# Narrow attentions of a six-block decoder: one pair of first scores in every step, the preparation turned by half a period, and the row maxima handed on in three groups

## The reference

```python
q, k = rope(x @ Wq), rope(src @ Wk)          # 32 heads of 16; 8 key heads (self) or 32 (cross)
s = q @ k.T                                  # 256 x 256 for each head; causal in self
attn = softmax(s / 4) @ (src @ Wv)
x = layernorm(x + attn @ Wo)                 # cross: + bout
```

## Time and profile before

| | |
|---|---|
| median of three runs | 3,955.1 us |
| profiled execution, device time | 3,946.1 us |
| its span in the profile | 3,944.4 us |
| granted clock of TensorE, mean over the span | 0.933 |
| TensorE matmuls busy | 3,485.5 us, 88% |
| VectorE busy | 1,760.1 us, 45% |
| ScalarE busy | 1,233.8 us, 31% |
| GpSimd busy | 287.2 us, 7% |
| the narrow attentions | from about 2,060 to 3,245 us of the span |

### The profile page before, as it was taken

How to read it: one execution, slowest core, us unless ns; L and a number is a source line. 1 busy time by engine, 2 the same in 40 slices (tenths; PEclk the granted TensorE clock), 3 DMA queues, 4 the chain that set the end, 5 groups by cost and what they waited for, 6 DMA issues and landing times. The chain is left out here.

```text
span 3944.4 us, 53071 instructions
## 1 busy us (share of the span) xinstructions
PE 3485.5 (88%) x18713; PEld 2422.7 (61%) x18714; DVE 1760.1 (45%) x5074; ACT 1233.8 (31%) x2714; POOL 287.2 (7%) x317
## 2 busy tenths in 40 slices
PE   7899999989999999977947898988888865999996
PEld 7666777756777777753424555544444434777774
DVE  4433444435444444431154545555555546334445
ACT  1222333323333333332112333334434434122111
POOL 2222000011000000023130000000000000000000
PEclk8999999999999999978967998999988877999998
DMA  6511111122111111123440000000000001000001
GB/s 238 187 38 38 53 48 48 45 94 86 46 45 43 45 45 45 32 111 135 133 133 1 2 2 2 18 10 18 4 5 7 1 25 41 11 21 11 11 21 43
DMA packets 83092, 191.62 MB, mean 49 GB/s; under 512 B 23424, under 2 KB 27520, under 8 KB 81864
## 3 DMA queue, kind: packets, MB, share of 16 engines
q0 software_dynamic: 32912, 100.03, 8.2%
q1 hardware_dynamic: 50048, 89.82, 6.6%
HBM read 138.30 MB, written 50.47 MB: 48 GB/s over the span
## 5 line engine op out<-in xcount | busy, mean ns | idle before, releaser
L1762 DVE TENSOR_REDUCE mx_n<-bank 128x6 f32<-128x768 f32 (+1 forms) x256 | 279.8, 1093 | 234.9 <-PE bank L1542 142.6
L1673 ACT ACTIVATE probsT_n<-bank 128x768 f32<-128x768 f32 (+1 forms) x256 | 235.9, 921 | 352.5 <-PE bank L1561 196.2
L1536 PE MATMUL bank<-kT_n,qT_n 48*128 48x256 f32 (+1 forms) x1024 | 143.4, 362 | 133.7 <-DVE mx_n L1762 131.5
L447 PE MATMUL bank<-wo_s,work_s 128*128 128x512 f32 x512 | 229.0, 598 | 6.3 <-ACT work_s L479 3.8
L447 PE MATMUL bank<-wo_x,work_x 128*128 128x512 f32 x512 | 227.2, 594 | 5.0 <-ACT work_x L479 3.8
L1536 PEld LDWEIGHTS bank<-kT_n,qT_n 48*128 48x128 f32 x1024 | 89.7, 213 | 211.8 <-DVE mx_n L1762 138.9
L479 ACT ACTIVATE work_s<-bank 128x512 f32<-128x512 f32 (+1 forms) x224 | 104.2, 465 | 353.9 <-PE bank L436 174.1
L479 ACT ACTIVATE work_x<-bank 128x256 f32<-128x256 f32 (+1 forms) x240 | 109.6, 460 | 322.6 <-PE bank L436 188.4
L584 DVE CUSTOM_DVE_ANT_0 work_x<-bank,work_x 128x256 f32<-128x256 f32 x256 | 97.8, 419 | 220.7 <-issue 220.7
L525 ACT ACTIVATE work_x<-work_x 128x256 f32<-128x256 f32 x256 | 128.3, 502 | 196.0 <-DVE work_x L589 196.0
L584 DVE CUSTOM_DVE_ANT_0 work_s<-bank,const 128x128 f32<-128x128 f32 (+1 forms) x256 | 80.8, 353 | 214.7 <-issue 214.7
(11 more groups left out here) (375 smaller groups left out, 7100.1 us busy)
## 6 DMA issues: line engine op xcount, KB each, us to landing
wq_lo_s<-wq_lo_s POOLq DMA_DIRECT2D x64, 512.0 KB, 3.6
wq_lo_x<-wq_lo_x POOLq DMA_DIRECT2D x64, 512.0 KB, 3.5
expert_rows<-table_zero SPq DMA_DIRECT2D x20, 512.0 KB, 14.2
work_m<-expert_rows SPq DMA_DIRECT2D x40, 256.0 KB, 2.6
expert_products<-work_m POOLq DMA_DIRECT2D x40, 256.0 KB, 2.7
expert_table<-table_zero SPq DMA_DIRECT2D x16, 512.0 KB, 14.1
weights_m<-expert_table SPq DMA_DIRECT2D x4, 2048.0 KB, 9.6
ug_rows<-in_L_ffn_W_gate SPq DMA_DIRECT2D x9, 512.0 KB, 3.6
```

The costliest lines, as they stand in the source:

```text
L447: last = pe.matmul(out[t][:, :], oT[:, h, t * P:(t + 1) * P], wo[:, h, :], start=(h == 0), stop=(h == H - 1), skip_group_check=True)
L1536: last = pe.matmul(out, q, kT[half(h, ROWS), n % 2, key_block(n, h), 0:keys], start=(t == 0), stop=cross(n), skip_group_check=True)
L1673: act.activation(probsT[:, turn_ % SLOT_PAIRS, :, 0:cols], scoreT[:, :, 0:cols], ACT.Exp, scale=SCALE)\
L1762: dve.tensor_reduce(to.rearrange("p t h -> p h t"), seen, AX.X, ALU.max).then_inc(s["scores_read"], 1)
```

## The change

`step` is rewritten. First scores: step `at` < 8 has pair `at` + 8 of the **current** item, step `at` >= 8 has pair `at` - 8 of the next one, so every step has one pair. Preparation moves about half an item: q, qT, kT11, kT12, kT13 and v of item n + 1 stay in item n, at steps 0 to 10; xT, ctxT, k, and the kT of item n + 2 now stand in steps 10 to 15 of item n. out0 and out1 of the last item move from steps 8 and 9 to 4 and 6, the norm stages from 10 to 13 to 7 to 10. The maxima go in three groups: pairs 0 to 5 (negA, step 14), 6 to 9 (negB, step 2 of the item), 10 to 15 (negC, step 8 of the item, first used in step 10). The prologue becomes seven units and 16 steps of an item -1, without second scores and values. The wait for the bias moves from VectorE's start to where it is used.

```diff
-        if at == 2:
-            a.append(("negB", n))
-        if g is not None:
-            whole = [x for x in ("kT02", "kT03", "kT12", "kT13") if cross(g)]
-            a += [(x, g) for x in {3: ["kT01"] + whole[0:1], 4: ["q0"] + whole[1:2], 5: ["kT11"] + whole[2:3],
-                                   6: ["qT00", "qT01"], 7: ["qT03", "qT10"], 10: ["qT12"], 11: ["v0"], 12: ["qT13"],
-                                   13: ["negA"]}.get(at, [])]
-            b += [(x, g) for x in {0: ["k0"], 1: ["k1"], 2: ["kT00"], 4: ["kT10"], 5: whole[3:4] + ["q1"], 6: ["qT02"],
-                                   7: ["qT11"], 12: ["v1"]}.get(at, [])]
-            if at >= 8:
-                a.insert(0, (2 * (at - 8), g))
-                b.insert(0, (2 * (at - 8) + 1, g))
...
+    GROUPS = ((0, 6), (6, 10), (10, PAIRS))
...
+        if at < 8:
+            put(a, now, [at + 8])
+        else:
+            put(a, g, [at - 8])
+        if at == 0:
+            put(a, f, ["h0", "h2"])
+            put(a, g, ["kT11"])
+            put(b, g, wide(g, "kT12", "kT13"))
+            put(b, g, ["q0"])
+        elif at == 1:
+            put(a, f, ["h1", "h3"])
+        elif at == 2:
+            put(a, now, ["negB"])
+            put(b, f, wide(f, "hT0", "hT1"))
+        elif at == 3:
+            put(a, g, ["q1"])
+        elif at == 4:
+            put(b, f, ["out0"])
+        elif at == 5:
+            put(a, g, ["qT00"])
+            put(b, g, ["qT01"])
+        elif at == 6:
+            put(b, f, ["out1"])
+        elif at == 7:
+            put(a, g, ["qT10"])
+            put(b, g, ["qT11", "qT02"])
+        elif at == 8:
+            put(a, now, ["negC"])
+            put(b, g, ["qT03", "qT12"])
+        elif at == 9:
+            put(a, g, ["v0"])
+            put(b, g, ["qT13"])
+        elif at == 10:
+            put(a, g, ["v1"])
+            put(b, e, ["xT0"])
+        elif at == 11:
+            put(a, e, ["xT1"])
+            put(b, e, wide(e, "ctxT"))
+        elif at == 12:
+            put(a, e, ["k0"])
+        elif at == 13:
+            put(a, e, ["k1"])
+        elif at == 14:
+            put(a, g, ["negA"])
+            put(b, e, ["kT00"])
+        elif at == 15:
+            put(a, e, ["kT01"])
+            put(a, e, wide(e, "kT02"))
+            put(b, e, wide(e, "kT03"))
+            put(b, e, ["kT10"])
...
+    before = [(x, 0) for x in ("xT0", "xT1", "k0", "k1", "kT00", "kT01", "kT10")]
...
-    mx, neg_hl = sb("mx", [P, 3, NH]), sb("neg_hl", [P, 2, TILES, 2, NH // 2])
-    negT = sb("negT", [P, 2, SEQ], FP32R)
+    mx, neg_hl = sb("mx", [P, 3, 3 * 12]), sb("neg_hl", [P, 3, TILES, NH])
+    negT = sb("negT", [P, 3, SEQ], FP32R)
...
-                for i, name in enumerate(("negA", "negB")):
+                for i, (name, (lo, hi)) in enumerate(zip(GROUP_NAMES, GROUPS)):
...
-                if pair % 8 == 0:
-                    pe.wait_ge(s["negA_there" if pair == 0 else "negB_there"], 64 * (n + 1))
+                if pair in (lo for lo, _ in GROUPS):
+                    pe.wait_ge(s[f"{GROUP_NAMES[group_of(pair)]}_there"], 64 * (n + 1))
...
-                if pair % 8 == 7:
-                    negate(n, pair // 8)
+                if pair == hi - 1:
+                    negate(n, i, 2 * other)
...
+            dve.memset(neg_hl[:, :, :, :], 0.0)
...
-                    if n >= 1 and at in (10, 11, 12, 13):
-                        norm_stage(at - 10, n - 1)
+                    if n >= 1 and at in (7, 8, 9, 10):
+                        norm_stage(at - 7, n - 1)
```

More of the change, by code:

```diff
@@ L1346, in attention_narrow @@
     turns = lambda n: range(4 if cross(n) else 2)
+    GROUPS = ((0, 6), (6, 10), (10, PAIRS))
+    GROUP_NAMES = ("negA", "negB", "negC")
+    group_of = lambda pair: [i for i, (lo, hi) in enumerate(GROUPS) if lo <= pair < hi][0]
     def step(n, at):
         f = n - 1 if n >= 1 else None
+        now = n if n >= 0 else None
         g = n + 1 if n + 1 < ITEMS else None
@@ L1371, in step @@
-        if e is not None:
-            a += [(x, e) for x in {14: ["xT0"]}.get(at, [])]
-            b += [(x, e) for x in {14: ["xT1"], 15: ["ctxT"] if cross(e) else []}.get(at, [])]
-        return a, b
[L1376 to L1379, removed]
@@ L1380, in attention_narrow, with put @@
-    after = order(ITEMS - 1, ["h0", "h2", "h1", "h3", "hT0", "hT1", "out0", "out1"])
-    whole = before + [u for n in range(ITEMS) for at in range(PAIRS) for slot in step(n, at) for u in slot] + after
+        def put(slot, item, names):
+            if item is not None:
+                slot.extend((x, item) for x in names)
+        wide = lambda item, *names: names if item is not None and cross(item) else ()
+        if at < 8:
+            put(a, now, [at + 8])
+        else:
+            put(a, g, [at - 8])
@@ L1382, in attention_narrow @@
+        return a, b
+    before = [(x, 0) for x in ("xT0", "xT1", "k0", "k1", "kT00", "kT01", "kT10")]
+    after = [(x, ITEMS - 1) for x in ("h0", "h2", "h1", "h3", "hT0", "hT1", "out0", "out1")]
+    whole = before + [u for n in range(-1, ITEMS) for at in range(PAIRS) for slot in step(n, at) for u in slot] + after
     uses = PrepOrder([u for u in whole if isinstance(u[0], str)])
@@ L1515, in prepare @@
                 else:
-                    i = "AB".index(name[3])
-                    pe.wait_ge(s["neg_ready"], 2 * n + i + 1)
+                    i = GROUP_NAMES.index(name)
+                    pe.wait_ge(s["neg_ready"], 3 * n + i + 1)
                     for t in range(TILES):
-                        last = pe.transpose(b[0:NH, t * P:(t + 1) * P],
-                                            neg_hl[:, i, t, :, :].rearrange("p l h -> p (l h)"), chip.ident)
+                        last = pe.transpose(b[0:NH, t * P:(t + 1) * P], neg_hl[:, i, t, :], chip.ident)
                 last.then_inc(s["prep_ready"], 1)
@@ L1617, in _ @@
                 emit(name, n)
-            for n in range(ITEMS):
+            for n in range(-1, ITEMS):
                 for at in range(PAIRS):
-                    second_scores(n, at)
+                    if n >= 0:
+                        second_scores(n, at)
                     early, late = step(n, at)
@@ L1687, in _ @@
                 evacuate(name, n)
-            for n in range(ITEMS):
+            for n in range(-1, ITEMS):
                 for at in range(PAIRS):
-                    exponentials(n, at)
+                    if n >= 0:
+                        exponentials(n, at)
                     early, late = step(n, at)
@@ L1843, in _ @@
                 do(name, n)
-            dve.wait_ge(s["bias_loaded"], 16)
-            for n in range(ITEMS):
+            for n in range(-1, ITEMS):
                 for at in range(PAIRS):
```

30 lines of the change are left out of this document (15 added, 15 removed).

## The result

| | before | changed |
|---|---|---|
| median of four runs, us | 3,954.5 | 3,847.7 |
| range, us | 3,944.4 to 3,961.7 | 3,835.6 to 3,849.6 |
| profiled execution, us | 3,946.1 | 3,847.9 |

A forecast was written before the change was run, and what follows sets the result against it. TensorE bounds the kernel, idling for the maxima and losing clock. Items 0 to 14 gain 92 us, with the prologue 109; 3,946.1 less 109 is 3,837, put at 3,840; range 3,805 to 3,875, with both neighbours 3,785 to 3,895.

The forecast's parts named there:

- Items 0 to 14: Steady part of the stage: 960 us against 1,052, a gain of 92 us.
- The walk of the waits: One pair per step, waits for maxima followed step by step: stalls 6.7 us per cross item; periods 64 cross, 59.5 self.
- The groups: Three groups of maxima, twelve row DMAs per item instead of eight: 0.3 us a mean item, bounds 0 and 1.5.
- The rest of the stage: Item 15 gets eight pairs of scores, taken to lie under its exponentials: 0 to +2 us.
- The prologue: Eight of sixteen pairs go, eight steps of some 3 us at low clock; item 0 starts near 2112: 17 us gained.
- The clock: TensorE's clock in the items: one fall per cross item, +4 us, and 1 us on a self item.
- That the clock stays up: Rival, chance 0.20: spread-out waits never lower TensorE's clock; gain 145 us, 3,801 us.
- VectorE as the pacemaker: Rival, chance 0.17: rotations between maxima delay everything behind, clock falls twice; self 64, cross 72; gain 54, 3,892 us.
- Slower: Rival, chance 0.03: waits of steps 2, 3, 14 and 15 keep the clock at 1.2 GHz; +97, 4,043 us.
- That it would not do what it says: Rival, chance 0.05: waits only change places, item times as now, the prologue alone gains; 3,929 us.
- The signs: Steady part: maxima wait 55 to 80 us, items about 60 and 68, clock above 0.91, item 0 near 2112.
- The sign of a low stretch over 13 us: Listed as showing the forecast wrong: stretches at low clock longer than 13 us.

The follow-up runs named there:

- e7_late: Changed kernel with the first scores of steps 2, 14 and 15 issued behind other units of the step; ratio 0.9772, 3,855.1 us.
- e8_late_split: Changed kernel with first scores late in steps 2, 14 and 15 and VectorE's rotations split around the next maxima; ratio 0.9796, 3,867.9 us.
- e2_two_groups: Changed kernel with the maxima handed on in two groups of eight pairs, negA in step 15, no negC; ratio 1.0235, 4,025.7 us.
- e1_pairs_only: Changed kernel keeping one pair per step and three groups, but preparation, out0/out1 and norm stages placed as before the change; ratio 0.9775, 3,841.7 us.
- e4_fill: Changed kernel with extra transposes rewriting the same values just ahead of the two long waits; ratio 0.9659, 3,794.9 us; repeated on another chip, 0.9683.
- e3_split: Changed kernel with VectorE's rotation split: bank-freeing multiplies, then the next step's maxima, then the rest; ratio 0.9682, 3,808.5 us.
- e5_split_after: Changed kernel with rotations split, the rest done behind the next step's maxima and other early units; ratio 0.9695, 3,827.7 us.

## Why the prediction was right, point by point

Forecast 3,840 us, in the range 3,785 to 3,895; measured 3,847.7. The terms:

- **Items 0 to 14**: forecast 960 us, measured 960. That it fits to the microsecond is luck. Items 0 to 5 took 369 us (forecast 363), items 6 and 7 134 (131), items 8 to 13 397 (408), item 14 61 (58): 12 us too little in one part and 11 too much in the other. It was also set against 1,052 us, where items 0 to 14 of the kernel before take 1,055.8 up to item 15's first second scores; the gain there is 96 us where 92 was forecast.
- **The walk of the waits** (part 1) was the step that carried it. Cross: forecast 2.6, 0.8 and 2.8 us in steps 2, 14 and 15, measured 2.95, 1.07 and 2.58. The 0.3 us in step 3 did not come in cross items. Self: forecast 1.8, 1.0 and 0.35, measured 1.78, 0.78 and 0.66; of the 0.55 us for negA's rows nothing came. The sum over items 0 to 14 was to be 55 to 80 us and is 70.6.
- **The groups** (part 3): twelve row DMAs an item cost nothing in the steady part, 0.4 us in one wait. The forecast 0.3 us an item was a little high. The Trainium skill (DMA: Bandwidth & Descriptors, Anatomy of one DMA) tells its fixed cost of some 2.0 us for the path through GpSimd, where these DMAs are issued by SyncE; worked out from it, as an estimate, 6 us more would have gone off the gain, and no steady item shows that wait. A wait for the rows does show twice at the end, at the start of item 15 and in its step 10:

```profile
3078.58 0.69 PE L1593 MATMUL bank<-qT_n,kT_n 50*128 50x256 f32 x4 [2.83 <-DMA qT_n<-negT_n]
...
3110.81 0.80 PE L1593 MATMUL bank<-qT_n,kT_n 50*128 50x256 f32 x4 [2.83 <-DMA qT_n<-negT_n]
```

- **The rest of the stage**: item 15 was forecast at 0 to +2 us, and the rest came out 8.9 us longer. The step that failed was to take the eight pairs of first scores as lying under the exponentials. TensorE's work there, at full clock, grew by 2.5 us, idle time by 3.1 us, nearly all of it the wait of step 10 for negC's rows, and low busy time by 6.8 us, half of which is 3.4. The cover of the DMAs had been counted in the steady part only: with no item left to prepare, steps 8 and 9 of item 15 have no qT and v units, and steps 14 and 15 of item 14 no kT units, so negC's and negA's rows are each waited for 2.83 us. (negA's wait ends where item 15 begins and counts with items 0 to 14.)
- **The prologue** (part 4) was mis-sized: forecast 17 us gained, measured 25.4. I priced the eight steps at the low clock of the old prologue's pairs, some 3 us each, 26 us. They took 19.8 us (2,098.77 to 2,118.59), the first six some 2 us each, and the clock there is 1.00 where it was 0.50 (a window of each, before and changed):

```profile
2100.00:2120.00 20.00, 11.40 (x54) 5.33 (x52) 8.22 (x11) 0.00 (x0) 0.00 (x0) 0.50 0.00 0
...
2100.00:2110.00 10.00, 8.96 (x77) 7.28 (x76) 5.67 (x11) 3.43 (x7) 0.00 (x0) 1.00 0.00 0
```

  In the old prologue TensorE waited for the maxima between the pairs (16.1 us in 15 waits); in the new one v, xT and k lie between them. Of the 25.4 us, 13.4 are idle time and 11.0 are half of the low busy time that went.
- **The clock** (part 5): about one fall per cross item and a small share in self items was the forecast. There are some 25 falls over the items, one or two per cross item and about one per self item, but short ones. In the steady cross items half of the low busy time is 3.8 us an item, where the forecast had 4; in self items 1 to 5 it is 2.7 us where the forecast had 1, and in item 0 it is 8.4 us. Over items 0 to 14 it is 50 us against a forecast of 36. The cross period was too long by its work: 57.8 us in the walk, 55.3 by the windows of 1.25 us. The self work was taken too short, 55.3 against 56.6 us.
- **The rivals.** That the clock stays up was wrong: it falls behind waits of 1.8 to 3 us, though not behind all of them. The Trainium skill (TensorE: Matmul & The Clock Gate, HAM oscillation) ties the fall to long idle gaps; by that rule the clock would have held in the steady part, where no wait for the maxima is over 3.3 us. The Trainium skill (TensorE: Matmul & The Clock Gate, A second HAM failure mode: psum-queue depth-cycling) also tells of a kernel in which short, frequent idle times between groups of matmuls made the clock go up and down; this trace, with 25 falls, agrees with that. VectorE as the pacemaker was wrong for the changed kernel, though in e7_late and e8_late_split moving the first scores back a little was enough to make TensorE wait more for VectorE's other results. Slower is what e2_two_groups did, by way of the DMAs and the clock. That it would not do what it says was wrong: the items themselves got shorter, not the prologue alone.
- **The signs.** In the steady part the wait fell to 70.6 us in 40 waits, its clock is 0.94, and no steady cross item is above 68 us. Item 0 starts 43.8 us into the stage, where the forecast had 51. The sign of a low stretch over 13 us did not come there, but it came in item 15: the clock is at 0.5 from about 3,105.6 to 3,130 us, and the DMA wait of step 10 lies inside (one window of that stretch):

```profile
3107.90:3127.80 19.90, 13.63 (x97) 6.91 (x96) 3.35 (x18) 8.71 (x11) 0.00 (x0) 0.50 0.01 2
```

- **The parts against each other.** The forecast did not price pairs and turn apart. e1_pairs_only shows 91 us for one and 21 for the other.

## What to carry to other kernels

When an engine waits in order on another one's queue, write down what stands in that queue at each step and walk one period: in the steady items it gave the place of each long wait and its size within 0.4 us. Walk the first and the last period too, where the units that cover a wait are missing. Price a wait of TensorE with the clock: here 97 us of idle time came with 61 us lost to 1.2 GHz, so each microsecond of idle time cost about 0.6 more (0.5 to 0.75 over the nine kernels without filling), and matmuls that do nothing but fill the waits paid for themselves. With the single score tile, refilling it first in the step did better than refilling it behind other work, which moved the wait to other units.

## What the runs showed that I had not expected

- TensorE does 38 us more work and the kernel is faster by 0.5 to 0.9% (e4_fill, 0.9659 and 0.9683 against 0.9733 and 0.9744). Nearly the same amount in another place cost 0.8 to 0.9% (0.9822).
- Less waiting is not less time: in e7_late the wait for the maxima fell from 72 to 48 us and the items grew by 16 to 20 us, by more low clock and by waits for other things.
- In e3_split 10 us of idle time went and the low busy time stayed at 129 us. In e5_split_after it is the other way about: against e3_split idle time rose by 4 us and the low busy time fell by 36 us. So the clock does not simply follow the sum of the waits, and behind the same wait of 1.8 us in the same step of a self item it falls in six items and not in the seventh. What exactly the clock answers to, these runs don't settle.
- The stage ahead, with unchanged code, began its successor anywhere from 2,043 to 2,076 us, in part by the chip; two profiled executions compared by their spans alone would be off by that much.
